# Cross-attention in a decoder layer: the value products of half a batch behind the next half batch's first scores

## What is computed

```python
q = x @ Wq.T; k, v = context @ Wk.T, ...   # 32 heads of 16
q = q * rsqrt(mean(q * q) + 1e-6); k = k * rsqrt(mean(k * k) + 1e-6)
attn = softmax(q @ k.T * 16 ** -0.5)
x = x + attn @ v
```

## Time and profile before

| what | value |
|---|---|
| median of 3 runs | 900.78 us (900.61 to 901.1) |
| the profiled execution | 900.3 us, of which the span from first to last instruction is 898.5 us |
| PE busy | 885.5 us, 99% of the span |
| DVE, ACT, POOL busy | 66%, 52%, 23% |
| granted PE clock, mean | 0.997 |
| the 48 steps | from 393.2 us to about 673 us of the span |

### The profile page before, as it was taken

How to read it: one execution, slowest core, us unless ns; L and a number is a source line. 1 busy time by engine, 2 the same in 40 slices (tenths; PEclk the granted TensorE clock), 3 DMA queues, 4 the chain that set the end, 5 groups by cost and what they waited for, 6 DMA issues and landing times.

```text
span 898.5 us, 17919 instructions
## 1 busy us (share of the span) xinstructions
PE 885.5 (99%) x7088; PEld 778.1 (87%) x7088; DVE 596.1 (66%) x1304; ACT 464.4 (52%) x1119; POOL 204.8 (23%) x147
## 2 busy tenths in 40 slices
PE   8999999999999999999999999999999999999995
PEld 8998989898989899877788888888877898999994
DVE  7886566666666635675665656646557878888883
ACT  5543333333333344547766666666675336656551
POOL 0143232323232215301101111011000621132233
PEclk9999999999999999999999999999999999999998
DMA  6221242424212115040200001000043688989973
GB/s 225 66 94 42 78 141 80 138 84 135 85 64 90 47 47 181 28 137 1 84 24 25 13 24 37 13 24 14 1 167 123 243 303 302 358 283 305 297 206 47
DMA packets 42195, 104.56 MB, mean 116 GB/s; under 512 B 8208, under 2 KB 18560, under 8 KB 40192
## 3 DMA queue, kind: packets, MB, share of 16 engines
q1 hardware_dynamic: 37808, 94.23, 30.7%
q0 software_dynamic: 4304, 9.19, 5.0%
HBM read 75.57 MB, written 18.65 MB: 105 GB/s over the span
## 4 chain that ended last, share of the span: by engine, by line
PE 96%; DVE 2%; ACT 0%; issue 0%; DMA 0%; POOL 0%; DVEq 0%
PE bank L595 25%; PE bank L596 24%; PE bank L597 24%; PE bank L852 5%; PE bank L869 5%; PE bank L695 3%; PE bank L671 3%; PE bank L683 1%; PE bank L711 1%; PE bank L812 1%; PE bank L981 1%; PE bank L879 1%; PE bank L989 1%; DVE pp L1745 0%; PE bank L819 0%
## 5 line engine op out<-in xcount | busy, mean ns | idle before, releaser
L1380 ACT ACTIVATE ee<-bank 125x448 f32<-125x448 f32 x192 | 90.8, 546 | 13.6 <-PE bank L852 13.6
L1628 DVE TENSOR_TENSOR E_lo<-F,E_hi 128x940 fp32r<-128x940 f32 (+3 forms) x62 | 80.8, 1320 | 2.2 <-ACT E_hi L1147 2.1
L595 PE MATMUL bank<-wkv_hi,ctx_hi 128*125 128x512 f32 x192 | 79.9, 416 | 0.0
L2330 POOL TENSOR_TENSOR ctx_lo<-ctx_f,ctx_hi 128x500 fp32r<-128x500 f32 x24 | 30.6, 1276 | 204.2 <-ACT ctx_hi L1147 204.2
L596 PE MATMUL bank<-wkv_hi,ctx_lo 128*125 128x512 f32 x192 | 76.2, 397 | 0.0
L597 PE MATMUL bank<-wkv_lo,ctx_hi 128*125 128x512 f32 x192 | 75.8, 395 | 0.0
L1147 ACT ACTIVATE E_hi<-F 128x940 fp32r<-128x940 f32 (+3 forms) x62 | 67.9, 1140 | 7.9 <-PE bank L597 3.6
L2330 POOL TENSOR_TENSOR wqk_lo<-wqk_f,wqk_hi 128x1024 fp32r<-128x1024 f32 x14 | 35.1, 2507 | 155.5 <-ACT wqk_hi L1147 155.5
L2440 POOL DMA_INDIRECT out<-yg,meta x21 | 39.5, 1880 | 126.1 <-DMA out<-yg,meta 72.1
L595 PE MATMUL bank<-wv_hi,xT_hi 128*128 128x256 f32 x224 | 63.5, 283 | 0.1
L597 PE MATMUL bank<-wv_lo,xT_hi 128*128 128x256 f32 x224 | 62.6, 279 | 0.0
(11 more groups left out here) (411 smaller groups left out, 2571.3 us busy)
## 6 DMA issues: line engine op xcount, KB each, us to landing
F<-wexp SPq DMA_DIRECT2D x14, 1408.0 KB, 7.7
F<-wexp SPq DMA_DIRECT2D x14, 768.0 KB, 6.9
wqk_f<-wqk SPq DMA_DIRECT2D x16, 512.0 KB, 4.3
ctx_f<-ctx SPq DMA_DIRECT2D x24, 250.0 KB, 2.8
slots<-zt SPq DMA_DIRECT2D x3, 1799.0 KB, 8.1
xg<-slots SPq DMA_DIRECT2D x21, 256.0 KB, 7.4
wv_f<-wv SPq DMA_DIRECT2D x8, 512.0 KB, 5.5
wo_f<-wo SPq DMA_DIRECT2D x8, 512.0 KB, 3.5
```

Source lines behind the costliest of these rows:

```text
L595: e.matmul(out, a[0], b[0], start=first, stop=False)
L1380: e.activation(ee[(4 * n + r) % 8][:, :], SX[r][0:MS, 0:4 * T], ACT.Exp, scale=0.25).then_inc(*x_exped.did((n, r)))
L1628: return e.tensor_tensor(out, src, high.bitcast(F32), ALU.subtract)
L2330: return e.tensor_tensor(out, src, high.bitcast(F32), ALU.subtract)
```

## The change

The three value blocks of a half batch are taken out of its steps. They now run together directly behind `score_pe` of the next half batch's first item (the last half batch's run at the end of step 47). `out_pe` moves behind the rows A of that step and ahead of the queries Q. On ACT `value_copy` moves behind the four exponentials of that step. On DVE `out_scale` moves behind `rows_sum` of A, and `out_add` and `third_stats` move behind `rows_sum` of Q, which is the last that DVE does in that step. The buffers `ee` grow from 8 to 12 and `vb` from 6 to 7. POOL sets the constant columns of the new `vb` buffer in step 0.

```diff
--- before.py
+++ after.py
@@ -32,6 +32,7 @@
 NA = 7
 NU = 2 * NB
 NK = MC * NU
+NEE, NVB = 4 * MC, 7
 ISQ = 1.0 / float(DH) ** 0.5
 LNE = 1e-5
 SC = KC * 256 + D
@@ -227,7 +228,8 @@
             ctx_f01.append(over(f"ctx_f{i}", [128, KC, MS], F32, room["mid"][0] - (4 * KC * MS + 31 & ~31)))
         assert room["mid"][0] <= place_v + NB * 256 * 4
         ctx = ctx[2:] + ctx[:2]
-        ee = [sbl(f"ee{i}", [MS, 4 * T], F32, "mid" if i < 6 else "z") for i in range(8)]
+        ee = [sbl(f"ee{i}", [MS, 4 * T], F32, "mid" if i < 6 else "z") for i in range(NEE)]
+        vb.append(sbl("vb6", [MS, XH, VW], F32, "z"))
         qT = [sbl(f"qT{i}", [128, 2, 2, T], F32, "mid") for i in range(2)]
         oo = [sbl(f"oo{i}", [128, 4 * T], F32, w) for i, w in enumerate(("mid", "mask"))]
         ss = [sbl(f"ss{i}", [MS, XH], F32, "free") for i in range(2)]
@@ -478,7 +480,7 @@
         stored = lane("out", [("rows", b) for b in range(NB)] + [*range(NA)])
         padded = lane("pad", [0])
 
-        consts_set = sig("consts_set", ["eps1", "zt", "zn", "eps"] + [("one", i) for i in range(12)] + [("route", i) for i in range(NE + NRB + 2)])
+        consts_set = sig("consts_set", ["eps1", "zt", "zn", "eps"] + [("one", i) for i in range(2 * NVB)] + [("route", i) for i in range(NE + NRB + 2)])
         mv_done = {n: sig(f"mv{n}", range(k)) for n, k in ((1, NA), (2, NB), (3, NB))}
         root_done = {n: sig(f"root{n}", range(k)) for n, k in ((1, len(FIRST)), (2, NB), (3, NB))}
         xn_done = {n: sig(f"xn{n}", range(k)) for n, k in ((2, NB), (3, NB))}
@@ -857,7 +859,7 @@
             def value_pe(n):
                 u, m = keys[n]
                 w.wait_ge(*squared[(u, m), "v"])
-                w.wait_ge(*consts_set["one", 11])
+                w.wait_ge(*consts_set["one", 11 if n < NVB - 1 else 2 * NVB - 1])
                 if m == 0:
                     if u:
                         w.wait_ge(*oo_done[u - 1])
@@ -866,10 +868,14 @@
                 for r in range(4):
                     w.wait_ge(*x_exped[n, r])
                     for c in range(4):
-                        i = e.matmul(AB[32 * c:32 * c + VW, r * T:(r + 1) * T], vb[n % 6][:, 8 * (c // 2) + 2 * r + c % 2, :],
-                                     ee[(4 * n + r) % 8][:, c * T:(c + 1) * T], start=m == 0 and r == 0,
+                        i = e.matmul(AB[32 * c:32 * c + VW, r * T:(r + 1) * T], vb[n % NVB][:, 8 * (c // 2) + 2 * r + c % 2, :],
+                                     ee[(4 * n + r) % NEE][:, c * T:(c + 1) * T], start=m == 0 and r == 0,
                                      stop=m == MC - 1, skip_group_check=True)
                     i.then_inc(*valued.did((n, r)))
+
+            def values_pe(u):
+                for m in range(MC):
+                    value_pe(MC * u + m)
 
             def out_pe(u):
                 x = ("o", u)
@@ -883,24 +889,24 @@
                 u, m = keys[n]
                 x = aside(n)
                 score_pe(n)
-                if x and x[0] == "o":
-                    out_pe(x[1])
-                elif x and x[0] == "n":
+                if m == 0 and u:
+                    values_pe(u - 1)
+                if x and x[0] == "n":
                     norm_turn(*x[1:])
-                elif x:
+                elif x and x[0] == "g":
                     gate_pe(*x[1:])
                 if n + 4 < NK:
                     rows_pe(*keys[n + 4])
                 else:
                     up_pe(0, (n - NK + 4) // 2, n % 2)
+                if x and x[0] == "o":
+                    out_pe(x[1])
                 if m == 0 and u + 1 < NU:
                     rows_pe(u + 1, "q")
                 if 0 < n < NK - 3:
                     rows_turn(keys[n + 3])
-                if m == MC - 1:
-                    value_pe(n - 1)
-                if m != 1:
-                    value_pe(n)
+                if n == NK - 1:
+                    values_pe(u)
                 if m == 1 and u + 1 < NU:
                     queries_turn(u + 1)
 
@@ -1360,10 +1366,10 @@
                 e.activation(sq[n % 2][0:R, :], KB[n % 2][0:R, 0:256], ACT.Square).then_inc(*squared.did(((u, m), "sq")))
                 if m != "q":
                     k = keys.index((u, m))
-                    if k > 5:
-                        w.wait_ge(*valued[k - 6, 3])
-                    w.wait_ge(*consts_set["one", 3 if k < 2 else 11])
-                    e.activation(vb[k % 6][:, :, 0:16], KB[n % 2][0:MS, 256:512].rearrange("p (h d) -> p h d", d=16),
+                    if k >= NVB:
+                        w.wait_ge(*valued[k - NVB, 3])
+                    w.wait_ge(*consts_set["one", 3 if k < 2 else 11 if k < NVB - 1 else 2 * NVB - 1])
+                    e.activation(vb[k % NVB][:, :, 0:16], KB[n % 2][0:MS, 256:512].rearrange("p (h d) -> p h d", d=16),
                                  ACT.Copy).then_inc(*squared.did(((u, m), "v")))
 
             def rows_root(u, m):
@@ -1375,9 +1381,9 @@
 
             def score_exp(n, r):
                 w.wait_ge(*scored_x[n, r])
-                if n > 1:
-                    w.wait_ge(*valued[n - 2, r])
-                e.activation(ee[(4 * n + r) % 8][:, :], SX[r][0:MS, 0:4 * T], ACT.Exp, scale=0.25).then_inc(*x_exped.did((n, r)))
+                if n >= MC:
+                    w.wait_ge(*valued[n - MC, r])
+                e.activation(ee[(4 * n + r) % NEE][:, :], SX[r][0:MS, 0:4 * T], ACT.Exp, scale=0.25).then_inc(*x_exped.did((n, r)))
 
             def value_copy(u):
                 w.wait_ge(*valued[MC * u + MC - 1, 3])
@@ -1411,6 +1417,8 @@
                     gate_copy(x[1])
                 score_exp(n, 2)
                 score_exp(n, 3)
+                if m == 0 and u:
+                    value_copy(u - 1)
                 for it in s_step.get(n, []):
                     s_hi_act(*it)
                 if i == 0 and n // 6 + 1 < NB:
@@ -1425,8 +1433,6 @@
                     rows_square(u + 1, "q")
                 if n == NK - 4:
                     gate_keep()
-                if m == MC - 1 and n < NK - 1:
-                    value_copy(u)
 
             def s_hi_act(c, part):
 
@@ -1974,16 +1980,10 @@
                     rows_finish(*keys[n + 3])
                 if m == 1 and u + 1 < NU:
                     rows_finish(u + 1, "q")
-                if x and x[0] == "o":
-                    out_scale(x[1])
-                elif x and x[0] == "n":
+                if x and x[0] == "n":
                     norm_low_x(*x[1:])
-                elif x and x[2] == 6:
+                elif x and x[0] == "g" and x[2] == 6:
                     gate_out(x[1])
-                if x and x[0] == "o":
-                    out_add()
-                    if i == 0:
-                        third_stats(b - 1)
                 if i == 0 and b + 1 < NB:
                     norm_out(2, b + 1)
                 if i == 1 and b:
@@ -1992,10 +1992,16 @@
                     s_low(*it)
                 if m == 0 and n + 4 < NK:
                     rows_sum(*keys[n + 4])
+                if x and x[0] == "o":
+                    out_scale(x[1])
                 if n + 3 < NK:
                     k_copy(*keys[n + 3])
                 if m == 0 and u + 1 < NU:
                     rows_sum(u + 1, "q")
+                if x and x[0] == "o":
+                    out_add()
+                    if i == 0:
+                        third_stats(b - 1)
                 if m == 1 and u + 1 < NU:
                     q_copy(u + 1)
                 if m and n + 4 < NK:
@@ -2401,6 +2407,8 @@
                 for k in ctx_step.get(n, []):
                     ctx_low(k)
                 if n == 0:
+                    w.wait_ge(*pj_full["o", NH // 2 - 1, NA - 1])
+                    ones(NVB - 1)
                     w.wait_ge(*gw_hi[0])
                     low(gw[1][:, :, :], gw_f[:, :, :], gw[0][:, :, :]).then_inc(*gw_lo.did(0))
```

## The result

The changed kernel takes 921.67 us (median of 5 executions, 918.35 to 925.54). The kernel before takes 900.89 us (5 executions). The ratio is 1.0231 (95% interval 1.0204 to 1.0257), so the change costs 2.3%. The profiled execution took 918.35 us, where the kernel before had 900.3.

The account below looks back on a forecast made before the run. TensorE was taken as the bound, with 96% of the chain that ended last. Waits of 18.4 us less 2.0 saved gave 16.4 on 900.3, so 916.7, plus 0.48 for the median: 917 us, range 909 to 921.

Parts of the forecast that it names:

- The direction and the mechanism: Whole kernel slower: without the value block as cover, TensorE waits for kn; 18.4 us lost, 2.0 saved.
- the place that was named: TensorE's weight load of the next rows after Q waits for DVE's kn, 15 times, 18 us in total.
- the half mechanism: Rival: cover is lost, but DVE's moved additions and statistics do not delay kn; 7.2 us lost, 906 us, 7%.
- The saving on PE: Two value groups become one per half batch on TensorE; net 0.13 us each, times 16, 2 us saved.
- Whoever is next: On TensorE the array must run empty behind the scores, whatever follows; 0.28 us.
- The rule of the Trainium skill: Value products fill all rows, so scores would drain in full before them; saving 1 us instead of 2.
- The clock: Rival: waits of 1.8 us drop TensorE's clock to 1.2 GHz, seven times; 29 us more, 946 us, 3%.
- my range: Whole kernel's time: main case 912 to 921 us, reached down to 909 toward the rival with smaller waits.
- the 4.2 that I had put down: Rows A and Q on TensorE, 4.2 us, would take twice as long after a clock fall, seven times.
- What cost nothing: Edits costed at nothing: moved out_pe, turn behind Q, value_copy behind the exponentials, POOL's two memsets.
- The slack of 0.1 us: At the turn behind Q, z_scaled ready 0.1 us early; if missed by 0.1, 15 times, 1.5 us added.
- the wait at B: B, TensorE's rows product in each second step, must wait for A's kn; 18.4 us lost in all.

Follow-up runs that it names:

- the last kernel of the third order: Against the kernel before: three value blocks together ending step m = 2, A's norm early, keys ahead of it, value copy behind the roots, third root early; 903.49 us, ratio 1.0035.

## Why the prediction was right or wrong

- **The direction and the mechanism were right.** The value block was the cover of the chain from Q's end over ACT's root of A to `kn`. The waits stand at the place that was named, fifteen of them, with the length that was worked out: 1.78 us for 1.79, 0.61 for 0.58, 2.15 for 2.17, 1.23 for 1.22, 0.85 for 0.83; in sum 18.6 for 18.4.
- **Shown by undoing it.** With the chain shortened and the order on PE kept, the time is 900.68 us. With the cover alone removed, there are 7.4 us of waits, where the half mechanism had 7.2. The rival in which only half of the mechanism acts is refuted by the full 18.6 of the changed kernel.
- **The saving on PE was mis-sized.** I took 2.0 us, with scores to values at the middle of 0.15 and 0.28. The start of the scores to the start of the values is 0.97 us (426.87 to 427.84), the same as to rows or turned results before, so this switch costs the full 0.28 us of an empty weight path and that part saves nothing. ("Whoever is next" was too wide: in the kernel before, the turn of the gate's result at `i = 5` starts 0.86 us behind the scores.) The weight loads of the values in after, then those of scores behind values in the kernel before:

```profile
427.84 2.27 PEld L871 LDWEIGHTS bank<-ee,vb 125*32 125x32 f32 x96 [0.28 <-issue]
```

```profile
434.04 0.69 PEld L852 LDWEIGHTS bank<-qT,kT 32*125 32x125 f32 x16 [0.17 <-issue]
```

  The rest came as worked out: a value group of 48 takes 2.43 us, that is 3 x 0.76 and 0.15 for the group, and Q's first product behind the turned results adds 0.09. Over the 48 steps about 1 us is saved. The rule of the Trainium skill that a weight load runs beside products in flight only when it is for another group of rows ("TensorE: Matmul & The Clock Gate", section "The mechanism") had given 1 us. The trace agrees with its price for this switch (0.28 us) and not with the rule as such: inside the value group the loads, all of them for the same 125 rows, run for 2.27 us beside products that follow one another without a gap. The missing saving is 1 us of the 1.65 between 916.7 and the profiled 918.35; the rest is 0.2 of longer waits and some 0.45 that I did not follow.
- **The clock was the step that failed.** The median of 921.67 is 0.7 us above my range, and it is 3.3 above the profiled execution, in which no fall stands in the steps and which lies inside the range. I put the clock at nothing in the sum and gave it 3%, as seven falls in every execution or none, from one stretch at the end of the kernel, where PE had stood idle for about 3 us at full clock. That row shows one stretch and not a limit. The runs showed a matter of more or less: in one of the two profiles of this kernel the 2.1 us wait was followed by a fall, its 28 shorter waits (up to 1.6 us of idle PE) were not, waits of 3.0 to 3.5 us were followed by one in six cases of seven, and in the profiles of the other kernels, whose longest wait in the steps is 1.6 us, none was seen. A fall costs 1.6 us, not the 4.2 that I had put down. The difference between the median and the profiled execution would be two falls. That is argued and not shown: it is worked out from the times, no profile of the median execution exists, and the mean clocks bear it out only roughly (0.003 lower, where two falls make 0.0037). It was in part luck that the median lay outside: the same kernel, measured again, gave 919.53 us, inside the range, with one fall seen in its profile. The Trainium skill's warning of waits between bursts that send the next burst back to the slow clock (same page, section "HAM oscillation — how this bites in real kernels") is borne out, in a small form.
- **What cost nothing, did.** The turn behind Q waited for `z_scaled` once, 0.3 us. The slack of 0.1 us held otherwise. ACT's later copy and POOL's memsets show in no wait of PE.

## What to carry to other kernels

Work that an engine does between two ends of a chain is cover, also where no wait shows; before it is moved, measure the slack of what comes behind it and compare it with the length of what is taken away (0.44 us of slack against 0.91). Work that moves to another place in the in-order queue of a second engine joins whatever chain runs through that place, and two such moves can cost more together than apart (18.6 us of waits against 7.4 and 6.8). On TensorE a wait of two or three microseconds can cost more than its length, because the clock can fall behind it; where it cannot be avoided, turns that compute nothing can be worth their instructions (10.1 us here).

## What the runs showed of the hardware that was not expected

- The fall of the clock behind waits of 2 to 3.5 us, its price of 1.6 us, and that 24 turns of 128 x 128 in such a wait prevent it (939.67 to 929.58 us).
- The switch from score products (four strips of 32 rows) to value products (four strips of 32 columns) costs the same 0.28 us of an empty weight path as rows or turned results behind the scores; from values to scores it is 0.17.
- A DVE instruction can be held for a microsecond by POOL. In the profile of after the scaling of rows took 1.52 us five times, once in each of batches 2 to 6, where the eleven others took 0.55. Each of the five started within 0.03 us of the split of the context on POOL and ended 0.28 us behind it. DVE first, then POOL:

```profile
469.65 0.16 DVE L1651 SCALAR_TENSOR_TENSOR rstd<-rt,rstd 112x1 f32<-112x1 f32 x1
469.85 1.52 DVE L1653 TENSOR_SCALAR xn<-xs,mv,rstd 112x512 f32<-112x512 f32 x1
```

```profile
469.82 1.27 POOL L2336 TENSOR_TENSOR ctx_lo<-ctx_f,ctx_hi 128x500 fp32r<-128x500 f32 x1 [17.45 <-ACT ctx_hi L1153]
```

  No wait of PE was followed back to it in this kernel. The kernel before has the same five, there on an instruction of 112 x 1 elements (1.03 us instead of 0.16). In the last kernel of the third order such an instruction took 1.14 us in the same company, in five cases of sixteen, again in batches 2 to 6. There `kn` of A starts 7.35 us behind the scores of its step, and 7.03 to 7.06 us in batches 1 and 7, where nothing is held. These 0.3 us are the rest of the wait at B. The comparison is between the batches of one profile; no run moved POOL's split away.
